# A smaller allowance for filler matmuls between attention units: the TensorE price of a unit in the credit rule goes from 3.6 N to 4.0 N

## The chip, the cores and the metric

The kernel runs on all 8 NeuronCores of one Trainium2 chip, each on one sequence of a batch of 8, with no traffic between cores. The metric is the device time in microseconds (us) of the slowest core. One profiled execution is looked at closely; its page and its finest views are those of core 7, the slowest.

## What is computed

The reference, cut to what matters (layernorm, softmax and silu are the usual ones; 16 heads of 64, sequence 2048, embedding 1024):

```python
xn = _layernorm(x, axis=-1)
q = shape_heads((xn @ wq.T + bq) * scaling)
k = shape_heads(xn @ wk.T + bk)
v = shape_heads(xn @ wv.T + bv)
scores = jnp.einsum('bhtd,bhsd->bhts', q, k)
mask = jnp.triu(jnp.full((T, T), -10000.0, dtype=jnp.float32), k=1)
attn = jax.nn.softmax(scores.astype(jnp.float32) + mask, axis=-1).astype(jnp.float16)
out = jnp.einsum('bhts,bhsd->bhtd', attn, v)
s = out.transpose(0, 2, 1, 3).reshape(B, T, E) @ wo.T + bo
g = _silu(jnp.einsum('bsd,od->bso', xn, weight) + pooled @ disha)
x = x + s * g
```

## The kernel before, in words

**Stages.** Each core first normalizes and transposes its 2048 rows, then runs the projections Q, K (line 345), V (line 370) and the gate g (line 394) as dense matmuls. Then comes attention, and behind it a drain. The change touches only what is issued from attention on.

**Attention.** The queries go in four blocks of 512 (`tc` 0 to 3). Each block runs over the 8 pairs of heads (`p`), and each pair over its chunks of 128 keys (`sc`): 4, 8, 12 and 16 chunks in blocks 0 to 3, since the mask is causal. One step (block, pair, chunk) is called a **unit** here; there are 32 + 64 + 96 + 128 = 320. A unit is a QK of two matmuls, one for each head (L643, L647), with N = 512 columns, or 384, 256 and 128 in the last three chunks of a pair; one exponential of both heads on ScalarE (L656, "exp" below), into one of 7 buffers PT; in the last four chunks a multiplication with the triangle on GpSimd (L665); and a PV of two matmuls (L682, L686), which TensorE issues five units later, out of a queue `pvq`. The QK results lie in two alternating PSUM slots, so QK of unit u waits for exp of unit u-2.

**The end of a pair.** Behind the last PV of a pair VectorE copies both heads' sums out (L575 OddA, L577 OddB), and the first PV of the next pair waits for the second copy, since it writes the same PSUM. SyncE moves the copies into AttnOT, and the softmax sums, one row for each head, into L16. After the eighth pair of a block VectorE takes the reciprocal of L16 (L611).

**The fillers.** Between the units TensorE gets pieces of two kinds of other work, which write the two PSUM slots of Q2. An **N tile** is one matmul (L462, 16 rows of contraction) that spreads the reciprocals, and a multiplication on VectorE that norms one pair's AttnOT (L471). An **E tile** is the output projection of 128 rows by 512 columns: eight matmuls (L505), one for the bias (L510, 1 row of contraction), then on VectorE times g (L520), plus x (L523), and the output DMA from GpSimd (L529) out of two alternating buffers `esb`. Each block has 8 N tiles and then 8 E tiles, and `fillq` holds them in that order, block by block. The N tiles of a block become ready with its reciprocal, its E tiles when its last N tile is done. The x rows for an E tile are loaded on SyncE's queue (L165) when the first E tile of the block is made.

**What sets the order.** The engines' instructions are written out in program order by this code; nothing reorders them at run time. After each unit a credit grows, and each time that it holds `CHUNK = 440.0`, `pop_chunk` takes one chunk: at most two matmuls of the current tile, so one chunk for an N tile and five for an E tile (four pairs and the bias alone). The credit is capped at `CCAP = 2600.0`. The multiplication, addition and output of a finished tile are issued when the next tile begins (`flush_pend`). What is left in `fillq` after the last unit runs in the **drain**:

```python
        while pvq:
            pvq.pop(0)()
            while lnq:
                lnq.pop(0)[1]()

        while fillq or FS["cur"] is not None:
            assert pop_chunk(), "filler not ready at drain"
```

The last reciprocal is thus in VectorE's order ahead of the evacuations of all tiles in the drain. It waits for DMAs that collect the last sums.

Of the kernel before, what the change touches and what calls it, by code (L numbers as in the profile page):

```python
# [44 lines left out]
def build_program(debug=False):  # L45
# [104 lines left out]
    with ExitStack() as ctx:  # L150
# [468 lines left out]
        for tc in range(NTC):  # L619
# [5 lines left out]
            for p in range(NPAIR):  # L625
                for sc in range(nsc):
# [7 lines left out]
                    N = 512 - off  # L634
# [60 lines left out]
                    if len(pvq) >= 5:  # L695
# [1 line left out]
                    pvq.append(pv_e)  # L697
                    u += 1
                    FS["credit"] = min(CCAP, FS["credit"]
                                       + (172.0 + 2 * N) / 1.2 - 3.6 * N / 2.4)  # L700
                    while FS["credit"] >= CHUNK:
                        if not pop_chunk():
                            break
# [104 lines left out]
```

How the kernel before makes its waits and increments, by code:

```python
def build_program(debug=False):  # L45
# [659 lines left out]
        while pvq:  # L705
            pvq.pop(0)()
            while lnq:
                lnq.pop(0)[1]()
        while fillq or FS["cur"] is not None:
            assert pop_chunk(), "filler not ready at drain"
        flush_pend()
        flush_pend()
        for i2 in range(2):
            S.emit("gpsimd", lambda g, i_=i2: g.wait_ge(sems[f"sO{i_}"], last_out[i_]))
        if debug:
            dma("sync", dbg["dbg_AOT"], AttnOT[:],
                waits=[("sDVE", tc_norm[3][0]), ("sSH0", sh_last[0])], sem="sDBG")
            gw = [(s, max((v for s2, v in g_done.values() if s2 == s), default=None))
                  for s in ("sACT", "sDVE")]
            dma("sync", dbg["dbg_g"], g_sb[:], waits=gw, sem="sDBG")
            S.emit("sync", lambda g: g.wait_ge(sems["sDBG"], S.cnt["sDBG"]))
        globals()["_last_cnt"] = dict(S.cnt)
        def run(eng, q):
            lastw = {}
            for fn, waits, inc, amt, _val in S.ops[q]:
                for (s, v) in waits:
                    if lastw.get(s, -1) >= v:
                        continue
                    eng.wait_ge(sems[s], v)
                    lastw[s] = v
                inst = fn(eng)
                if inc is not None:
                    inst.then_inc(sems[inc], amt)
```

## Time and profile before

| | us |
|---|---|
| two timed runs | 778.58 and 806.78 (median 792.68) |
| the profiled execution, whole | 781.28 |
| its span, slowest core (7) | 779.7 |
| spans of the 8 cores | 758.3 to 779.7 |
| PE (TensorE) busy on core 7 | 653.0 |
| ACT (ScalarE) busy | 341.4 |
| DVE (VectorE) busy | 251.7 |

### The profile page before, as it was taken

The numbers are of one execution on the slowest core, as the hardware profiler recorded it, in microseconds if no ns is written. First come the engines' busy times: TensorE is split into PE (matmuls) and PEld (weight loads), VectorE is DVE, ScalarE is ACT, GpSimd is POOL, SyncE is SP. The second block draws the span as 40 slices with busy tenths as digits, with TensorE's granted clock in tenths as the row PEclk, the third lists the DMA queues.
The fourth block names the chain that finished last, engine by engine and source line by source line (L and its number), as shares of the span: only waits on it lengthen the run. The fifth ranks groups of instructions, "written<-read, shape, count | busy, mean of one in ns | idle before, by whom it ended". The sixth has DMA issues, their size and how long they took to land.

```text
span 779.7 us, 8775 instructions; the slowest of 8 cores (758.3 to 779.7 us)
## 1 busy us (share of the span) xinstructions
PE 653.0 (84%) x2784; PEld 238.2 (31%) x2784; DVE 251.7 (32%) x372; ACT 341.4 (44%) x387; POOL 103.1 (13%) x164
## 2 busy tenths in 40 slices
PE   0543999999999999777688889998999899988665
PEld 0433444444333444221122222222222222222211
DVE  5856644444333100022422323222213321222154
ACT  0322000000000233655257788657789858888400
POOL 0000000000000000343022313111131211111201
PEclk9999999999999999755568999659799959999868
DMA  6322410110100000300020111020001120110122
GB/s 199 90 64 67 156 55 1 55 54 7 49 1 0 1 0 1 115 22 21 7 68 28 30 39 48 20 62 28 21 32 38 34 62 21 35 34 21 42 67 95
DMA packets 25696, 34.86 MB, mean 45 GB/s; under 512 B 4898, under 2 KB 19362, under 8 KB 25652
## 3 DMA queue, kind: packets, MB, share of 16 engines
q1 hardware_dynamic: 23092, 25.91, 11.6%
q0 software_dynamic: 2560, 8.39, 2.8%
q8 instruction: 24, 0.39, 0.2%
q14 instruction: 20, 0.16, 0.1%
HBM read 21.63 MB, written 8.39 MB: 39 GB/s over the span
## 4 chain that ended last, share of the span: by engine, by line
PE 73%; DVE 15%; DMA 4%; issue 4%; ACT 1%; SPq 1%; DVEq 1%; POOL 0%; POOLq 0%; ACTq 0%
PE PS L682 14%; PE PS L345 13%; PE PS L643 12%; PE PS L686 9%; PE PS L370 8%; PE PS L394 7%; PE Q L505 6%; DVE OddB L577 3%; DVE OddA L575 3%; DVE xn L233 2%; DVE st L208 1%; DVE st L210 1%; DMA xin<-x 1%; PE Q L462 1%; PE PS L373 1%
## 5 line engine op out<-in xcount | busy, mean ns | idle before, releaser
L656 ACT ACTIVATE PT<-PS,neg 128x1024 f16<-128x1024 f32 (+1 forms) x320 | 300.5, 984 | 113.1 <-PE PS L647 109.0
L665 POOL TENSOR_TENSOR PT<-PT,tri 128x256 f16<-128x256 f16 x128 | 85.9, 677 | 633.1 <-ACT PT L656 628.5
L682 PE MATMUL PS<-PT,Vp 128*65 128x512 f16 (+1 forms) x320 | 135.1, 422 | 41.0 <-DVE OddB L577 40.8
L643 PE MATMUL PS<-QT,KT 64*128 64x512 f16 (+1 forms) x320 | 126.8, 397 | 9.0 <-ACT PT L656 7.9
L686 PE MATMUL PS<-PT,Vp 128*65 128x512 f16 (+1 forms) x320 | 129.7, 405 | 0.0
L647 PE MATMUL PS<-QT,KT 64*128 64x512 f16 (+1 forms) x320 | 127.3, 399 | 0.0
L345 PE MATMUL PS<-xnT,wsb 128*128 128x512 f16 x512 | 112.3, 382 | 0.8 <-DVE QT L355 0.8
L575 DVE CAST OddA<-PS 65x512 f16<-65x512 f32 x32 | 22.0, 687 | 222.4 <-PE PS L686 205.0
L400 ACT ACT_TABLE_LOAD x1 | 1.3, 1283 | 182.4 <-PE PS L394 182.4
L505 PE MATMUL Q<-woT,AttnOT 128*128 128x512 f16 x256 | 77.4, 402 | 1.4 <-DVE AttnOT L471 1.1
L643 PEld LDWEIGHTS PS<-QT,KT 64*128 64x128 f16 x320 | 30.2, 94 | 144.3 <-issue 144.3
L682 PEld LDWEIGHTS PS<-PT,Vp 128*65 128x65 f16 x320 | 36.5, 114 | 117.6 <-issue 112.3
L241 PE MATMUL PS<-eye,xn 128*128 128x128 f32 x128 | 31.0, 424 | 49.1 <-ACT xnT L250 34.6
L345 PEld LDWEIGHTS PS<-xnT,wsb 128*128 128x128 f16 x512 | 50.4, 99 | 62.3 <-issue 3.2
L370 PE MATMUL PS<-wsb,xnT 128*128 128x512 f16 x256 | 60.8, 380 | 0.0
L520 DVE TENSOR_TENSOR esb<-Q,g 128x512 f32<-128x512 f32 x32 | 22.1, 692 | 105.7 <-PE Q L510 71.7
L394 PE MATMUL PS<-Weff,xnT 128*128 128x512 f16 x256 | 55.4, 379 | 0.0
L241 PEld LDWEIGHTS PS<-eye,xn 128*128 128x128 f32 x128 | 25.1, 223 | 54.6 <-issue 54.6
L686 PEld LDWEIGHTS PS<-PT,Vp 128*65 128x65 f16 x320 | 39.6, 124 | 0.3
L382 DVE CAST Vp<-PS 128x512 f16<-128x512 f32 x32 | 22.2, 695 | 46.4 <-PE PS L373 46.4
L505 PEld LDWEIGHTS Q<-woT,AttnOT 128*128 128x128 f16 x256 | 25.1, 101 | 30.4 <-issue 9.7
L394 PEld LDWEIGHTS PS<-Weff,xnT 128*128 128x128 f16 x256 | 25.0, 98 | 30.2 <-issue 0.2
(39 smaller groups left out, 349.4 us busy)
## 6 DMA issues: line engine op xcount, KB each, us to landing
out<-esb POOLq DMA_DIRECT2D x32, 256.0 KB, 2.4
xin<-x SPq DMA_DIRECT2D x16, 256.0 KB, 3.8
wbig<-wT SPq DMA_DIRECT2D x8, 512.0 KB, 6.7
QT<-x SPq DMA_DIRECT2D x32, 128.0 KB, 2.3
wsb<-wqT SPq DMA_DIRECT2D x2, 1024.0 KB, 8.6
wsb<-wkT SPq DMA_DIRECT2D x2, 1024.0 KB, 5.2
wsb<-wvT SPq DMA_DIRECT2D x2, 1024.0 KB, 5.3
woT<-woT SPq DMA_DIRECT2D x1, 2048.0 KB, 10.8
```

Source lines behind the costliest of these rows:

```text
L241: p_tp[tt] = S.emit("tensor", lambda g, jj=j, p=tt % 2: g.transpose(PS6[:, 4 + jj // 4, (jj % 4) * NP:(jj % 4 + 1) * NP], xn_sb[p][:, jj * ...
L345: g.matmul(ps, wsb[w][:, ec_, o_ * NP:(o_ + 1) * NP], xnT[:, ec_, t_ * 512:(t_ + 1) * 512], start=first, stop=last))
L370: g.matmul(ps, xnT[:, ec_, t_ * NP:(t_ + 1) * NP], wsb[w][:, ec_, :], start=first, stop=last))
L394: g.matmul(ps, xnT[:, ec_, t_ * NP:(t_ + 1) * NP], Weff[:, ec_, h * 512:(h + 1) * 512], start=first, stop=last))
L505: S.emit("tensor", lambda g: g.matmul(psF[sl], AttnOT[:, pc_, t_ * NP:(t_ + 1) * NP], woT[:, pc_, o * 512:(o + 1) * 512], start=first, sto ...
L575: evA = S.emit("vector", lambda g: g.tensor_copy(OddA[0:65, :], PS6[0:65, 4, :]), waits=wr, inc="sDVE")
L643: g.matmul(PS6[:, 2 * par_ + 0, o:o + n], KT[0:64, p_, sb2:sb2 + NP], QT[0:64, p_, t + o:t + 512], start=True, stop=True),
L647: g.matmul(PS6[:, 2 * par_ + 1, o:o + n], KT[64:128, p_, sb2:sb2 + NP], QT[64:128, p_, t + o:t + 512], start=True, stop=True),
L656: g.activation(PT[sl_][:, :, o:o + n], PS6[:, 2 * par_:2 * par_ + 2, o:o + n], AF.Exp, bias=neg2[:]), waits=we, inc="sACT")
L665: g.tensor_tensor(PT[sl_][:, :, o:o + NP], PT[sl_][:, :, o:o + NP], t, ALU.mult),
L682: S.emit("tensor", lambda g: g.matmul(psO(0, 65, 0, o, o + n), Vp[:, s_, (2 * p_) * 65:(2 * p_) * 65 + 65], PT[sl_][:, 0, o:o + n], start= ...
L686: pv = S.emit("tensor", lambda g: g.matmul(psO(0, 65, 1, o, o + n), Vp[:, s_, (2 * p_ + 1) * 65:(2 * p_ + 1) * 65 + 65], PT[sl_][:, 1, o:o ...
```

## The change

One number changes: the matmul columns that a unit is charged with.

```diff
                     FS["credit"] = min(CCAP, FS["credit"]
-                                       + (172.0 + 2 * N) / 1.2 - 3.6 * N / 2.4)
+                                       + (172.0 + 2 * N) / 1.2 - 4.0 * N / 2.4)
```

The first term stands for the unit's exponential, the second for its matmuls, both in ns. Before, a unit adds 228.7, 207.3, 186.0 or 164.7 (N = 512, 384, 256, 128); now it adds 143.3 whatever N is. So a pair of block 3 is given 8.0 chunks before and 5.2 now, one of block 2 5.9 and 3.9, one of block 1 3.9 and 2.6. All the work remains; its places change.

In TensorE's order before, inside block 3, a filler (L505 x2) stands two units after the one ahead of it:

```order
1280 L505 MATMUL Q<-woT,AttnOT 128x512 x2
1281 L643 MATMUL PS<-QT,KT 128x512
1282 L647 MATMUL PS<-QT,KT 128x512
1283 L682 MATMUL PS<-PT_61,Vp 65x512
1284 L686 MATMUL PS<-PT_61,Vp 65x512
1285 L643 MATMUL PS<-QT,KT 128x512
1286 L647 MATMUL PS<-QT,KT 128x512
1287 L682 MATMUL PS<-PT_62,Vp 65x512
1288 L686 MATMUL PS<-PT_62,Vp 65x512
1289 L505 MATMUL Q<-woT,AttnOT 128x512 x2
```

In TensorE's order of the change, in the same block, three units follow on a filler before the next one, which is the row L510 directly below these:

```order
1272 L505 MATMUL Q<-woT,AttnOT 128x512 x2
1273 L643 MATMUL PS<-QT,KT 128x512
1274 L647 MATMUL PS<-QT,KT 128x512
1275 L682 MATMUL PS<-PT_61,Vp 65x512
1276 L686 MATMUL PS<-PT_61,Vp 65x512
1277 L643 MATMUL PS<-QT,KT 128x512
1278 L647 MATMUL PS<-QT,KT 128x512
1279 L682 MATMUL PS<-PT_62,Vp 65x512
1280 L686 MATMUL PS<-PT_62,Vp 65x512
1281 L643 MATMUL PS<-QT,KT 128x512
1282 L647 MATMUL PS<-QT,KT 128x512
1283 L682 MATMUL PS<-PT_63,Vp 65x512
```

Fillers have moved apart, from every second unit to every third.

TensorE's order at the end of attention before: behind the last PV come the 8 N tiles and then the 8 E tiles of block 3.

```order
1504 L682 MATMUL PS<-PT_110,Vp 65x128
1505 L686 MATMUL PS<-PT_110,Vp 65x128
1506 L462 MATMUL Q<-L_57,hsel 128x512 x8
1507 L505 MATMUL Q<-woT,AttnOT 128x512 x8
1508 L510 MATMUL Q<-bo_sb,ones_76 128x512
```

The same place in the change, first the beginning of the drain and then its middle:

```order
1458 L682 MATMUL PS<-PT_110,Vp 65x128
1459 L686 MATMUL PS<-PT_110,Vp 65x128
1460 L462 MATMUL Q<-L_57,hsel 128x512 x6
1461 L505 MATMUL Q<-woT,AttnOT 128x512 x8
1462 L510 MATMUL Q<-bo_sb,ones_76 128x512
```

```order
1475 L505 MATMUL Q<-woT,AttnOT 128x512 x8
1476 L510 MATMUL Q<-bo_sb,ones_76 128x512
1477 L462 MATMUL Q<-L_57,hsel 128x512 x8
1478 L505 MATMUL Q<-woT,AttnOT 128x512 x8
1479 L510 MATMUL Q<-bo_sb,ones_76 128x512
```

Six N tiles and all eight E tiles of block 2 now stand in the drain, ahead of those of block 3.

Over the whole of attention TensorE now has 18 N tiles and 16 E tiles between its units where it had 24 and 24. The N tiles of block 1 stood at units 128 to 142 (one at each second) and now stand at units 172 to 192 (one at each third); those of block 2 stood at units 225 to 238, and now two stand at the end of block 3 and six in the drain.

VectorE's order at the end of attention before:

```order
228 L575 CAST OddA<-PS 65x512
229 L577 CAST OddB_85<-PS 65x512
230 L611 RECIPROCAL L_57<-L_57 16x512
231 L471 TENSOR_TENSOR AttnOT<-AttnOT,Q 128x512 x8
232 L520 TENSOR_TENSOR esb_47<-Q,g 128x512
```

And in the change:

```order
211 L575 CAST OddA<-PS 65x512
212 L577 CAST OddB_85<-PS 65x512
213 L611 RECIPROCAL L_57<-L_57 16x512
214 L471 TENSOR_TENSOR AttnOT<-AttnOT,Q 128x512 x7
215 L520 TENSOR_TENSOR esb_47<-Q,g 128x512
```

The evacuations of the moved tiles stand behind the last reciprocal; the first L471 among them belongs to an N tile whose matmul is still inside attention. On SyncE's queue the 8 loads of x for block 2 (L165) move from the middle of block 3 to the end, next to the 8 for block 3.

## Rows read from the trace of the kernel before

**Rows 1.** The cores view: span and mean granted clock of a core.

```profile
core 5: 758.6 us, clock 0.920
core 7: 779.7 us, clock 0.890
```

**Rows 2.** TensorE's timeline, core 7, at the full clock: start, duration, engine, line.

```profile
480.12 0.39 PE L510 MATMUL Q<-bo_sb,ones 1*128 1x512 f16 x1
480.44 0.39 PE L643 MATMUL PS<-QT,KT 64*128 64x512 f16 x1
...
485.03 0.38 PE L686 MATMUL PS<-PT,Vp 128*65 128x512 f16 x1
485.35 0.39 PE L643 MATMUL PS<-QT,KT 64*128 64x512 f16 x1
...
485.91 0.38 PE L686 MATMUL PS<-PT,Vp 128*65 128x512 f16 x1
486.12 0.59 PE L505 MATMUL Q<-woT,AttnOT 128*128 128x512 f16 x2
486.65 0.39 PE L643 MATMUL PS<-QT,KT 64*128 64x512 f16 x1
```

**Rows 3.** ScalarE's timeline, core 7, behind the end of a pair.

```profile
668.28 2.12 ACT L656 ACTIVATE PT<-PS,neg 128x1024 f16<-128x1024 f32 x2 [1.24 <-PE PS L647]
```

**Rows 4.** TensorE's timeline, core 7, at the lower clock.

```profile
407.01 0.63 PE L686 MATMUL PS<-PT,Vp 128*65 128x512 f16 x1
407.44 1.06 PE L505 MATMUL Q<-woT,AttnOT 128*128 128x512 f16 x2
408.43 0.60 PE L643 MATMUL PS<-QT,KT 64*128 64x512 f16 x1
...
409.39 0.63 PE L686 MATMUL PS<-PT,Vp 128*65 128x512 f16 x1
409.96 0.60 PE L643 MATMUL PS<-QT,KT 64*128 64x512 f16 x1
```

**Rows 5.** Stretches of core 7: length, busy time of each engine, PEclk, DMA.

```profile
100.00:300.00 200.00, 200.00 (x897) 84.79 (x896) 64.88 (x87) 13.86 (x23) 0.00 (x0) 1.00 0.07 22
320.00:380.00 60.00, 40.73 (x146) 10.71 (x146) 16.37 (x20) 30.79 (x39) 23.21 (x35) 0.51 0.17 50
490.23:510.37 20.14, 18.74 (x54) 4.00 (x54) 5.51 (x9) 12.25 (x14) 3.17 (x5) 0.55 0.06 20
510.37:528.95 18.58, 17.04 (x57) 4.24 (x57) 4.12 (x7) 11.37 (x13) 2.67 (x4) 0.66 0.22 64
540.00:548.00 8.00, 6.10 (x23) 1.72 (x22) 2.76 (x4) 5.21 (x6) 0.00 (x0) 0.72 0.09 20
574.57:587.81 13.24, 12.13 (x59) 3.86 (x59) 2.76 (x5) 11.32 (x13) 3.68 (x6) 1.00 0.14 50
623.30:648.12 24.82, 23.28 (x75) 5.50 (x75) 5.50 (x9) 16.31 (x18) 2.66 (x4) 0.66 0.17 48
684.00:701.89 17.89, 16.34 (x78) 5.17 (x78) 4.14 (x7) 15.51 (x18) 3.68 (x6) 1.00 0.11 37
```

**Rows 6.** A stretch of core 5: from OddB of one pair to OddB of the next.

```profile
628.86:646.74 17.88, 16.34 (x78) 5.16 (x78) 4.14 (x6) 15.56 (x18) 3.15 (x5) 1.00 0.07 23
```

**Rows 7.** The timeline of the drain, core 7.

```profile
740.54 3.34 DVE L611 RECIPROCAL L<-L 16x512 f16<-16x512 f16 x1 [3.71 <-DMA L<-OddB]
...
744.85 6.25 DVE L471 TENSOR_TENSOR AttnOT<-AttnOT,Q 128x512 f16<-128x512 f16 x8 [0.97 <-PE Q L462]
...
751.35 3.57 PE L505 MATMUL Q<-woT,AttnOT 128*128 128x512 f16 x8 [1.12 <-DVE AttnOT L471]
...
755.34 1.90 PE L505 MATMUL Q<-woT,AttnOT 128*128 128x512 f16 x8
...
764.17 1.89 PE L505 MATMUL Q<-woT,AttnOT 128*128 128x512 f16 x8 [0.17 <-DVE esb L520]
...
768.69 1.89 PE L505 MATMUL Q<-woT,AttnOT 128*128 128x512 f16 x8 [0.16 <-DVE esb L520]
```

## The prediction, made before the changed kernel was run

> **What bounds the kernel now.** Look first at the cores [rows 1]: the same program takes 758.6 us on core 5 and 779.7 on core 7, and the slower one has the lower mean clock. So TensorE is near enough to the limit that its clock shows in the time, and the kernel's time is that of the core whose clock fell most.
>
> Then at one unit at the full clock. From an L686 to the next QK it is 0.32 us without a filler (485.03 to 485.35), and 0.56 later comes the next L686 (485.91): a unit with N = 512 costs TensorE 0.88 us [rows 2]. ScalarE's exp of such a unit takes 2.12 / 2 = 1.06 us [rows 3]. Without fillers ScalarE would set the pace. A pair of L505 lengthens the step from L686 to QK from 0.32 to 0.74 us, so it costs 0.42; a single L510 (and, by the same row, an L462) costs its 0.32 [rows 2]. With one chunk in about two units, four in five of them pairs, TensorE needs 0.88 + 0.52 x 0.40 = 1.09 us a unit, only 0.03 over ScalarE's pace. The two engines are almost balanced.
>
> Last at the pairs of heads. One of block 3 takes 17.89 us at the full clock on core 7, and 17.88 on core 5, with ScalarE busy 15.51 and idle 2.4 [rows 5, 6]. Half of that idle time is one gap of 1.24 us at the pair's end [rows 3]. With the clock down the same 16 units took 24.82 us [rows 5].
>
> **The change, part by part.** Eight E tiles (32 pairs of L505, 8 single L510) and six N tiles (6 single L462) leave attention for the drain: 46 chunks.
>
> *What attention gains.* At the full clock, if TensorE kept the pace, 32 x 0.42 + 14 x 0.32 = 17.9 us [rows 2]. ScalarE's pace lies close under it, so not all can be had. In a pair of block 3 the 2.8 chunks removed are 1.1 us of TensorE's time. The 13 long units can give 0.03 each, 0.4; the rest must come out of ScalarE's idle 2.4 us: the gap at the pair's end, when no filler stands in it any more, and the three short units, whose exps are shorter than TensorE's work. I take 0.9 to 1.0 of the 1.1, or 85%: 15 us. At the lower clock a pair of L505 costs 1.42 - 0.57 = 0.85 us [rows 4], twice as much, and TensorE alone sets the pace. By core 7's mean clock of 0.890 some 170 us of its span were at the lower level [rows 1]; block 0, before the first filler, has 59 of them [rows 5] and the drain a part, so I estimate that a fifth of the chunks lie in such stretches: 0.2 x 18 = 4 us more. Together -19 us. Bounds: -12, if only the long units' 0.4 and half of the rest come; -26, if half of the chunks removed had stood at the lower clock.
>
> *What the drain pays.* Nothing but its own DMAs runs beside it, so all of it is on the path. VectorE reaches the moved evacuations only behind the reciprocal, which waits for the last sums: the 3.71 us of that wait and the 3.34 of L611 are not filled [rows 7], except by the matmul or two that fit in the two PSUM slots. Behind it:
> - Seven L471 of block 2's N tiles at 6.25 / 8 = 0.78: 5.5, less the 0.97 that the first now waits for its matmul [rows 7]: 4.5 us.
> - The first E tile at the lower clock, 755.34 - 751.35 = 4.0, and seven at (768.69 - 764.17) / 2 = 2.26, the pace of the two output buffers [rows 7]: 19.8.
> - Block 3's first L471 then waits for the last E tile's L520 and L523: about 1.5.
>
> Sum +26 us. Bounds: 23, if the first tile runs at the full clock and TensorE's 1.90 + 0.32 a tile is the pace; 30, if the clock falls again among these tiles. Block 3's own tiles cost what they did. The 16 loads of x, now in a row on SyncE, are issued while VectorE waits for the reciprocal and then works through N tiles; I cost them at nothing, since the second eight are wanted only 26 us later, and the first eight have the reciprocal and 5.5 us of L471 to land in. In the middle of block 3 eight loads disappear from ahead of OddA's and OddB's DMAs, for which nobody waits there: nothing.
>
> On a limit by current the trace says this: through 200 us of dense matmuls on eight cores PEclk is 1.00 [rows 5]. The Trainium skill (TensorE: Matmul & The Clock Gate, Part 1, Seeing it yourself) says that once three cores of a die run dense matmuls a limiter takes the clock to 13/16. By it each of the eight moved tiles would take some 2.7 us in the denser drain, 3 to 4 us more in all; the trace disagrees, and the sum doesn't need it.
>
> *The clock.* This is the term that no row prices directly. With N tiles as fillers the clock stays down: 20.14 and 18.58 us for pairs of block 2 at 0.55 and 0.66, against 13.24 for one at 1.00, an excess of 12 us; at block 2's N tiles in block 3 24.82 instead of 17.88 us, 6.9 us, on core 7 but not on core 5 [rows 5, 6]. With none (block 0) it is 0.51, and one fall came in block 2 among E fillers, with 0.72 in its 8 us [rows 5]. The clock comes back around E fillers: the steps at 407 to 410 are at the lower clock, L505 among them [rows 4], those at 485 at the full one [rows 2]. So full-height fillers hold the clock up, and the change thins them from one chunk in two units to one in three. Against that, attention's own matmuls then come a little faster, and only one stretch of N tiles is left inside blocks 2 and 3 instead of two, 21 units long instead of 14. I price: the second stretch gone, -7; the first longer by half of its excess, +6; one or two more falls among E fillers on the slowest core at 3 to 7 us each, +7. Sum +6 us. Bounds: -10 (no such falls, a quick recovery) and +35 (half of the 24 pairs lose 3 us each).
>
> **Sum.** 781.28 (the profiled execution, 1.6 us more than its span) - 19 + 26 + 6 = 794; I say 793 us, 1.5% more than before. The two runs of before are 778.58 and 806.78; the profiled one agrees with the lower, and the median 792.68 is only their middle. My percentages are against 781. About 2%, to 797 or 766, is what a measurement of this kernel can tell from no change.
>
> **The rivals.**
> - *The clock gives way.* At one chunk in three units the falls at the pairs' ends become the rule. For it: block 0's 0.51 and the fall at 540 [rows 5], at a denser filling than will be. Against it: the pairs late in block 3 hold 1.00 [rows 5, 6]. A pair of block 3 that loses the clock loses up to 6.9 us; if a third to a half of the 24 pairs of blocks 1 to 3 lose 3 us on average, that is 24 to 36 instead of my 7: 810 to 822.
> - *ScalarE swallows the gain.* If its idle time at the pairs' ends doesn't shrink, since OddB's copy and not the filler sets it, a pair gives back only the long units' 0.4, some 8 us in all, and 4 of the lower clock: 781 + 26 - 12 + 6 = 801, or 796 with half of the clock's term.
> - *Faster.* The second N stretch leaves attention and takes the slowest core's fall with it; fewer matmuls among the rest do no harm. Core 5, which never fell there, ended 21 us earlier [rows 1]. If every core becomes like core 5: 758.6 + 1.6 + 26 - 15 = 771, and with the first N stretch no more costly than now and gains at pair ends in full, 765. It decides at the point where thirds of fillers still hold the clock.
> - *The change doesn't do what it says.* The order shows the tiles in the drain; no chance.
>
> **How the numbers follow.** The forecast, 785 to 797: 0.46. The clock gives way: 0.30. ScalarE swallows the gain: 0.12, of which 0.08 over the line of 797. Faster: 0.12, of which 0.07 under 766. So slower by over 2% 0.38, within 2% 0.46 + 0.04 + 0.05 = 0.55, faster 0.07. The range, 770 to 824, takes in all but the far end of the first rival and the larger part of the last.
>
> **What the changed profile would show.** From L611's start to the end of the span 39.2 us before (779.7 - 740.54); 64 to 67 if the drain's price is right. A pair of block 3 at the full clock 16.8 to 17.1 us instead of 17.89, with ScalarE idle 1.3 to 1.6. Seven L471 behind L611 without a gap. In the granted clock one long low stretch, in the last part of block 2, instead of two; and at the pairs' ends elsewhere either no more falls than now, or many. I am wrong if the pairs at the full clock don't shorten (ScalarE), if the moved tiles run at under 2 us each or hide in the wait for the reciprocal, or if the slowest core's mean clock moves by more than 0.02: 0.02 of the span is 31 us more or less at the lower level, where a pair takes 1.39 times as long, some 9 us.

## The result, and the profile after

The change makes the kernel slower by half a per cent: 783.79 us against 779.65 (medians of 30 and 29 runs), and the ratio of the comparable runs is 1.0053, with a 95% interval of 1.0035 to 1.0071. The direction was the forecast one, the size was not: +4 us instead of +12. The profiled executions are 779.75 us for the change and 781.28 before, one 4 us under its median and one 1.6 over, so the traces are compared part by part and not by their ends. (On every chip some executions run with part of the cores at a lower granted clock for long, 0.75 through the dense matmuls in one of delay_3_6, an experiment below; they are left out, and so are cores 6 and 7 of delay_only below.)

The cores of the changed kernel; these are its slowest and fastest:

```profile
core 1: 778.2 us, clock 0.916
core 2: 772.1 us, clock 0.918
```

Before, they lay between 758.6 and 779.7 [rows 1]. The spread has shrunk from 21 us to 6: the mean of the eight spans rose by 6.3 us (768.8 to 775.1), the slowest hardly moved.

From the starts of L577, the copy at each pair's end, every core's span splits into blocks (from the eighth such start, the end of block 0, to the sixteenth and so on) and the part behind the last one. Means over the eight cores, in us:

| | block 1 | block 2 | block 3 | sum | behind the last OddB |
|---|---|---|---|---|---|
| before | 90.8 | 123.0 | 145.0 | 358.8 | 43.3 |
| change | 92.2 | 108.3 | 136.0 | 336.5 | 71.6 |
| difference | +1.4 | -14.7 | -9.0 | -22.3 | +28.3 |

So attention gave back 22 us, and the drain took 28, in these two executions.

The drain, VectorE's timeline on core 1:

```profile
710.86 3.34 DVE L611 RECIPROCAL L<-L 16x512 f16<-16x512 f16 x1 [3.71 <-DMA L<-OddB]
714.30 5.46 DVE L471 TENSOR_TENSOR AttnOT<-AttnOT,Q 128x512 f16<-128x512 f16 x7
724.43 0.69 DVE L520 TENSOR_TENSOR esb<-Q,g 128x512 f32<-128x512 f32 x1 [4.67 <-PE Q L510]
...
741.48 0.69 DVE L520 TENSOR_TENSOR esb<-Q,g 128x512 f32<-128x512 f32 x1 [1.31 <-DMA out<-esb]
...
743.07 6.25 DVE L471 TENSOR_TENSOR AttnOT<-AttnOT,Q 128x512 f16<-128x512 f16 x8
```

The wait of 3.71 us ahead of L611 is as long as before [rows 7]. Seven L471 follow without a gap, then eight E tiles whose evacuations start at 724.43 for the first and 741.48 for the last, 2.44 us apart; only then come block 3's eight L471. From L611 to the end it is 67.3 us (778.2 - 710.86), where it was 39.2.

TensorE's timeline in the same stretch shows the clock within it:

```profile
720.01 3.57 PE L505 MATMUL Q<-woT,AttnOT 128*128 128x512 f16 x8 [1.11 <-DVE AttnOT L471]
724.05 2.60 PE L505 MATMUL Q<-woT,AttnOT 128*128 128x512 f16 x8
726.90 1.90 PE L505 MATMUL Q<-woT,AttnOT 128*128 128x512 f16 x8
...
737.65 1.90 PE L505 MATMUL Q<-woT,AttnOT 128*128 128x512 f16 x8
...
749.58 3.46 PE L505 MATMUL Q<-woT,AttnOT 128*128 128x512 f16 x8 [1.12 <-DVE AttnOT L471]
```

The first eight matmuls take 3.57 us, at the lower level, the second eight still 2.60, and the clock is lost once more while block 3's N tiles run, so the price of a restart is paid twice.

Attention on core 1, pair by pair (from OddB to OddB; after the five engines' busy times comes PEclk):

```profile
487.59:500.66 13.07, 11.44 (x56) 3.68 (x56) 2.76 (x5) 11.10 (x14) 2.58 (x4) 1.00 0.04 10
526.59:540.96 14.37, 12.77 (x54) 3.67 (x54) 2.77 (x5) 11.43 (x13) 3.68 (x6) 0.88 0.14 47
553.54:569.93 16.39, 14.56 (x55) 3.72 (x55) 4.13 (x7) 11.74 (x14) 2.62 (x4) 0.79 0.30 74
569.93:588.31 18.38, 16.81 (x73) 4.87 (x73) 6.10 (x5) 15.49 (x18) 3.03 (x4) 0.91 0.03 8
605.33:624.02 18.69, 17.21 (x75) 5.04 (x75) 2.76 (x4) 15.45 (x17) 3.15 (x5) 0.91 0.07 22
657.68:674.77 17.09, 15.39 (x73) 4.78 (x73) 2.75 (x5) 15.24 (x17) 3.11 (x5) 1.00 0.08 25
```

At the full clock a pair of block 3 now takes 17.09 us with ScalarE busy 15.24, against 17.89 [rows 5]. The three long pairs of before, 20.14, 18.58 and 24.82 us at 0.55 to 0.66 [rows 5], have no counterpart in blocks 2 and 3 of this core. The lowest there is the last pair of block 2, at 0.79, in which the one N stretch ends. On core 0, alone of the eight, that pair is still a long one:

```profile
552.45:571.26 18.81, 17.27 (x55) 4.05 (x55) 4.13 (x6) 11.98 (x14) 2.67 (x4) 0.64 0.25 64
```

What came instead are short falls, pairs at 0.88 to 0.91 that lose some 1.5 us. The first pair of block 1 is as it was, 21.47 us at 0.54 on core 1 against 22.01 at 0.50 on core 7 before; what it holds comes out below.

### The profile page after: what moved, and what is told of

Its sections match the earlier page's. It is cut to its first block, busy times and chain, and to the rows that moved or that the text cites. A ratio compares the mean times of both kernels' runs of the same rounds, so it can differ in the third digit from the quotient of the medians.

```text
span 778.2 us, 8777 instructions; the slowest of 8 cores (772.1 to 778.2 us)
## 1 busy us (share of the span) xinstructions
PE 639.3 (82%) x2784; PEld 237.4 (31%) x2784; DVE 251.5 (32%) x372; ACT 335.9 (43%) x387; POOL 102.4 (13%) x164
## 4 chain that ended last, share of the span: by engine, by line
PE 66%; DVE 16%; DMA 5%; issue 5%; ACT 4%; SPq 1%; DVEq 1%; POOL 0%; ACTq 0%; POOLq 0%
PE PS L345 13%; PE PS L682 12%; PE PS L643 10%; PE PS L370 8%; PE PS L686 8%; PE PS L394 7%; PE Q L505 5%; ACT PT L656 4%; DVE OddB L577 3%; DVE OddA L575 3%; DMA out<-esb 2%; DVE AttnOT L471 2%; DVE xn L233 2%; DMA xin<-x 2%; DVE st L208 1%
## 5 line engine op out<-in xcount | busy, mean ns | idle before, releaser
L656 ACT ACTIVATE PT<-PS,neg 128x1024 f16<-128x1024 f32 (+1 forms) x320 | 295.0, 989 | 88.1 <-PE PS L647 86.1
L682 PE MATMUL PS<-PT,Vp 128*65 128x512 f16 (+1 forms) x320 | 128.7, 402 | 41.4 <-DVE OddB L577 41.3
L643 PE MATMUL PS<-QT,KT 64*128 64x512 f16 (+1 forms) x320 | 120.9, 379 | 13.4 <-ACT PT L656 11.2
L686 PE MATMUL PS<-PT,Vp 128*65 128x512 f16 (+1 forms) x320 | 122.8, 384 | 0.0
L647 PE MATMUL PS<-QT,KT 64*128 64x512 f16 (+1 forms) x320 | 121.9, 382 | 0.0
L505 PE MATMUL Q<-woT,AttnOT 128*128 128x512 f16 x256 | 75.6, 411 | 3.3 <-DVE AttnOT L471 2.5
L682 PEld LDWEIGHTS PS<-PT,Vp 128*65 128x65 f16 x320 | 35.8, 112 | 112.9 <-issue 107.3
L686 PEld LDWEIGHTS PS<-PT,Vp 128*65 128x65 f16 x320 | 38.0, 119 | 0.4
L505 PEld LDWEIGHTS Q<-woT,AttnOT 128*128 128x128 f16 x256 | 25.0, 103 | 35.4 <-issue 16.0
```

Source lines behind the costliest of these rows:

```text
L505: S.emit("tensor", lambda g: g.matmul(psF[sl], AttnOT[:, pc_, t_ * NP:(t_ + 1) * NP], woT[:, pc_, o * 512:(o + 1) * 512], start=first, sto ...
L643: g.matmul(PS6[:, 2 * par_ + 0, o:o + n], KT[0:64, p_, sb2:sb2 + NP], QT[0:64, p_, t + o:t + 512], start=True, stop=True),
L647: g.matmul(PS6[:, 2 * par_ + 1, o:o + n], KT[64:128, p_, sb2:sb2 + NP], QT[64:128, p_, t + o:t + 512], start=True, stop=True),
L656: g.activation(PT[sl_][:, :, o:o + n], PS6[:, 2 * par_:2 * par_ + 2, o:o + n], AF.Exp, bias=neg2[:]), waits=we, inc="sACT")
L682: S.emit("tensor", lambda g: g.matmul(psO(0, 65, 0, o, o + n), Vp[:, s_, (2 * p_) * 65:(2 * p_) * 65 + 65], PT[sl_][:, 0, o:o + n], start= ...
L686: pv = S.emit("tensor", lambda g: g.matmul(psO(0, 65, 1, o, o + n), Vp[:, s_, (2 * p_ + 1) * 65:(2 * p_ + 1) * 65 + 65], PT[sl_][:, 1, o:o ...
```

## The experiments

Theory A, from these rows: a filler with all 128 rows of contraction (L505) brings TensorE's clock back and a low one (16 rows in L462, 1 in L510) doesn't; the change gained in attention by shortening the long low stretches, and not because thinner fillers are cheap. The rivals: the clock falls by the gap at a pair's end, whatever fills (D); the gain comes from the thinner fillers themselves (H). The drain's price is told apart from all of that by moving one instruction.

Where the clock falls and rises can be read from the kernel before, on core 7. At the end of a pair TensorE waits 1.26 us for OddB and works on; some 1.5 us later its clock falls, and it stays down over the two pairs with N tiles:

```profile
491.06 0.38 PE L682 MATMUL PS<-PT,Vp 128*65 128x512 f16 x1 [1.26 <-DVE OddB L577]
```

```profile
491.00:492.00 1.00, 0.94 (x5) 0.33 (x5) 0.00 (x0) 0.27 (x1) 0.00 (x0) 1.00 0.00 0
492.00:493.00 1.00, 1.00 (x4) 0.14 (x2) 0.69 (x1) 0.60 (x1) 0.00 (x0) 0.70 0.45 113
493.00:494.00 1.00, 1.00 (x4) 0.29 (x4) 0.69 (x1) 0.71 (x2) 0.00 (x0) 0.50 0.09 20
...
522.00:523.00 1.00, 1.00 (x3) 0.15 (x1) 0.00 (x0) 0.00 (x0) 0.67 (x1) 0.50 0.00 0
523.00:524.00 1.00, 1.00 (x5) 0.23 (x4) 0.00 (x0) 0.32 (x1) 0.00 (x0) 0.94 0.00 0
```

It comes back at 523, behind the first pair of L505 that follows the N tiles:

```profile
522.20 1.05 PE L505 MATMUL Q<-woT,AttnOT 128*128 128x512 f16 x2
```

In blocks 2 and 3 of this core and of core 1 of the change there are nine falls. Each begins 0.7 to 2.5 us after the start of L577 at the end of a pair.

Times in the table are medians, with the ratio to the kernel before on the same chip.

| kernel | us | ratio (95%) | block 1 | block 2 | block 3 | behind |
|---|---|---|---|---|---|---|
| price_3_2 | 787.06 | 1.0116 (1.006 to 1.0172) | 91.9 | 120.2 | 155.5 | 43.8 |
| price_4_4 | 809.59 | 1.0393 (1.0297 to 1.0488) | 90.6 | 123.4 | 134.5 | 84.4 |
| n_full | 773.6 | 0.9936 (0.9903 to 0.9969) | 93.3 | 114.2 | 145.9 | 46.1 |
| n_low | 790.67 | 1.011 (0.9973 to 1.0246) | 92.9 | 122.9 | 146.1 | 45.6 |
| interleave | 773.34 | 0.994 (0.9902 to 0.9978) | 91.5 | 115.3 | 149.0 | 43.3 |
| delay_inter | 753.6 | 0.9688 (0.9586 to 0.9791) | 85.0 | 108.5 | 139.1 | 48.3 |
| delay_only (time: delay_3_6) | 758.18 | 0.9756 (0.9699 to 0.9814) | 83.6 | 111.9 | 139.1 | 44.3 |
| delay_4_0 | 781.19 | 1.0069 (1.0043 to 1.0095) | 87.1 | 114.9 | 134.7 | 70.6 |
| late_recip | 776.83 | 1.0003 (0.9966 to 1.0039) | 92.8 | 108.9 | 135.8 | 64.8 |
| all_4_0 | 773.79 | 0.9975 (0.9933 to 1.0017) | 87.4 | 112.9 | 135.5 | 65.3 |
| mix_3_8 | 761.04 | none | 83.7 | 106.9 | 137.1 | 57.0 |
| n_full_4_0 | 788.67 | none | 95.2 | 109.8 | 134.6 | 74.5 |

The parts are means over the eight cores of the profiled execution, for delay_only over cores 0 to 5; they are compared with the one profile of the kernel before, from another chip. The time and ratio in delay_only's line are those of delay_3_6, the same kernel. mix_3_8 and n_full_4_0 have no ratio, and their time is that of the profiled execution alone.

### More and less credit

```diff
-                                       + (172.0 + 2 * N) / 1.2 - 3.6 * N / 2.4)
+                                       + (172.0 + 2 * N) / 1.2 - 3.2 * N / 2.4)
```

> More credit, 314 ns for a long unit, 0.71 chunks. Attention can't hold more than the 144 chunks that it had before, so they come earlier and the end of each block of units runs without fillers until the next reciprocal. Part behind the last OddB 43 us as before. Theory A: in the stretches without fillers the clock falls, as with N tiles, so blocks 2 and 3 together take as long as before or up to 10 us more (268 to 278 us), time 778 to 790. Theory B gives the same sign. Rival C (the clock plays no part, ScalarE against TensorE is all): units with fillers 1.17 us, units without 1.06, sum unchanged, time within 3 us of before.

787 us, 1.2% slower. Block 2 takes 120 us and block 3 155.5, 10 more than before, with the drain unchanged. The numbers are inside what A said, but not for A's reason. These are the first pair of block 3 on core 1 and one late in the block, which has no filler at all:

```profile
578.00:609.80 31.80, 24.74 (x85) 6.14 (x85) 11.60 (x14) 16.09 (x17) 3.21 (x5) 0.68 0.14 38
682.92:700.32 17.40, 15.11 (x64) 4.16 (x64) 1.37 (x2) 15.24 (x17) 2.59 (x4) 0.90 0.03 8
```

The fillers ran out 15 units before the end of block 2, and then five N tiles in a row waited for the reciprocal, 4.93 us in one piece. That first pair alone is 14 us longer than before. The pair without fillers has only a short fall, so in block 3 the clock doesn't stay down for want of fillers (in block 0, which has none either, it is at 0.51 [rows 5]).

With 4.4 in the same place:

> Half as many chunks again leave attention: 58 ns of credit for a long unit and up to 122 for a short one, some 51 chunks in attention in all instead of 98. Theory A (TensorE's clock is held up by full-height fillers and falls where they are missing; one chunk in three units was still enough): one in seven is not enough, pairs at the full clock are at ScalarE's pace (16.5 us in block 3, against 16.9 with 4.0), but the clock falls at most pair ends and block 3 takes over 145 us instead of 136. Theory B (the clock falls only where N tiles or nothing fill, and any E filler holds it): block 3 takes 132 to 134 us. The part behind the last OddB grows from 71.6 by 47 chunks, some 9 tiles of 2.3 us plus N tiles, to 95 to 98. Time: A 810 to 825, B 795 to 800.

3.9% slower. A is wrong about block 3, and B, which had 132 to 134 us for it, comes within half a us of the 134.5 measured. Neither had the rest: the part behind grows only to 84.4 us, because block 3 can't start before block 1's N tiles are done: the code forces 26 chunks in between, and the last pair of block 2 takes 30 us on core 1. In block 3, with one filler in seven units, a pair at the full clock is down to 16.4 us, ScalarE's pace with its gap. Core 1, its first and third pair there:

```profile
575.38:593.02 17.64, 15.72 (x68) 4.44 (x68) 4.72 (x4) 15.08 (x16) 2.58 (x4) 0.90 0.03 8
...
611.21:627.60 16.39, 14.34 (x68) 4.35 (x68) 2.76 (x5) 15.23 (x17) 2.58 (x4) 1.00 0.04 9
```

So thin fillers cost falls of 1.2 to 3 us at the ends of three or four of block 3's eight pairs, and no collapse. And beyond 4.0 there is little left to win: 16.4 against 17.0 us a pair.

### Is it the filler's height?

n_full, in the N tile of the kernel before:

```diff
+                S.emit("tensor", lambda g: g.matmul(
+                    psF[sl], woT[:, 0, 0:NP], woT[:, 0, 0:512],
+                    start=True, stop=True), waits=pw_ + [("sWO", c_wo)])
                 pval = S.emit("tensor", lambda g: g.matmul(
```

> The kernel before, with one additional matmul of 128 rows by 512 columns ahead of each N tile's matmul of 16 rows, into the same PSUM slot, overwritten by it: 32 more matmuls, 24 in attention, 0.21 us each at the full clock, some 5 us of TensorE's time. Theory A (low fillers let the clock fall, full-height ones hold it): the falls at the N tiles of blocks 1 and 2 go, block 2 takes 110 to 114 us instead of 117 to 125, block 3 139 to 141 on every core instead of 148 on most; time 8 to 12 us less than before. Rival D (it falls by the gap at the pair's end, whatever fills the units): block 2 and 3 unchanged or 2 us longer each, time +3 to +5.

n_low has the N tile's own 16-row matmul in that place instead:

> Control for n_full: the kernel before, with each N tile's own matmul of 16 rows issued twice instead of once behind a matmul of 128 rows. The same number of matmuls with the same columns, but low ones. Theory A (it is the height of the filler that holds TensorE's clock): block 2 takes 117 to 125 us on the cores and block 3 140 to 149, as before, and the part behind the last OddB 46; time 3 to 6 us more than before. Rival E (any matmul more between the units holds it): block 2 114 us as in n_full, time 5 us less than before.

With the high one block 2 falls from 123.0 to 114.2 us, with the low one it stays at 122.9. Both kernels have the same number of matmuls with the same columns. The pair with the N stretch and the one behind it on core 1, n_full:

```profile
487.82:503.47 15.65, 14.11 (x59) 4.02 (x59) 5.51 (x8) 11.65 (x14) 3.15 (x5) 0.89 0.08 26
503.47:517.53 14.06, 12.52 (x60) 4.01 (x60) 4.12 (x6) 11.33 (x13) 2.63 (x4) 1.00 0.30 84
```

and n_low:

```profile
492.05:512.08 20.03, 18.48 (x59) 3.96 (x59) 5.51 (x8) 11.87 (x14) 3.17 (x5) 0.66 0.06 21
512.08:530.59 18.51, 16.96 (x60) 4.21 (x60) 4.12 (x7) 11.54 (x13) 2.67 (x4) 0.72 0.21 64
```

Seven of n_full's eight cores have the same two pairs to 0.05 us. In n_low one of the two or both are at 0.56 to 0.72, on every core. So in block 2 the height tells and the mere number doesn't. But a high filler doesn't bring the clock back each time. On core 0 of n_full the first of these pairs, and on core 7 the pair with the second N stretch, are as long as those of before or longer:

```profile
488.81:508.90 20.09, 18.54 (x59) 4.52 (x59) 5.51 (x9) 11.86 (x14) 3.17 (x5) 0.66 0.07 21
```

```profile
611.57:639.04 27.47, 25.92 (x80) 6.27 (x80) 5.50 (x9) 16.12 (x17) 2.66 (x4) 0.63 0.14 43
```

On core 7 the clock stood at 0.50 from 614 to 633 us, with a full-height matmul ahead of each of the N tiles in between, and came back behind the first pair of L505 (L508 there), as before. In block 3 neither kernel gave what A said: 145.9 and 146.1 us. Its pair with the second N stretch takes 20.1 to 27.5 us in n_full, in n_low 20.1 on five cores and 29.0 on three, in the kernel before 17.5 on three and 24.8 on five. So there the height isn't shown to do anything. n_full's time fell by 0.6%, half of what was expected. That is the slowest core's: the mean of the eight spans over its comparable executions is 766.2 us, against 766.7 before and 776.5 for n_low, whose two such executions leave its ratio unclear.

In n_full_4_0 the same edit stands in the change:

> The change (4.0) with n_full's edit: a full-height matmul ahead of each N tile's low one. In the change one N stretch is left inside blocks 2 and 3, in the last two pairs of block 2, and block 2 has 7.0 us above eight times its shortest pair. Theory A (height holds the clock): that excess falls to 2 to 4, block 2 takes 103 to 105 us; blocks 1 and 3 as in the change (92 and 136); time 1 to 4 us less than that of the change, since 14 of the 32 additional matmuls are in the drain. Rival F (the excess in the change is from its thin E fillers, not from the N tiles): block 2 stays at 107 to 109, time 1 to 3 us more than the change.

Block 2 takes 109.8 us instead of 108.3, nearer to F, with an excess over the shortest pairs of 5.4 to 6.6 us on four cores and 10.9 to 12.0 on the other four. So in the change the 7 us in the last pairs of block 2 are not cured by high N fillers. The cause is open.

### N tiles between E tiles

interleave takes an N tile between two chunks of an E tile, when one is ready, from `pop_chunk`; its core is:

```diff
+            if FS["cur"] is not None and FS["cur_kind"] == "E":
+                k = next((i for i, e_ in enumerate(fillq) if e_["kind"] == "N"), None)
+                if FS["alt"] and k is not None and fillq[k]["ready"]():
...
+                    em_n = mk_n_tile(fillq.pop(k))[0]
```

> The kernel before with its credit; the N tiles of a block are not issued in a row, but one by one between the chunks of the E tiles of the block before that are still left, so that an N tile stands at most at every fourth unit. The same matmuls in attention and drain. Theory A: no stretch without full-height fillers is left behind block 1's, so block 2 takes 106 to 110 us (eight pairs of 13.25), block 3 139 to 141 on all cores; time 10 to 14 us less than before. Rival D: no change, within 3 us.

0.6% faster, again half of the expectation. Block 2 gains 8 us, block 3 loses 4. The two long stretches are gone from core 1, but new ones stand at the first pair of blocks 2 and 3:

```profile
460.44:480.03 19.59, 13.91 (x57) 3.94 (x57) 7.47 (x7) 11.35 (x13) 3.20 (x5) 0.83 0.03 7
480.03:493.45 13.42, 11.87 (x57) 3.71 (x57) 3.44 (x6) 11.52 (x14) 2.62 (x4) 1.00 0.10 31
...
574.82:599.73 24.91, 18.64 (x76) 5.22 (x76) 8.17 (x9) 16.11 (x18) 3.66 (x5) 0.86 0.05 17
```

In the first, TensorE is busy 13.91 of 19.59 us, which a low clock doesn't explain: it stands still, for the reciprocal (L623 here):

```profile
468.32 0.58 PE L462 MATMUL Q<-L,hsel 16*128 16x512 f16 x1 [4.28 <-DVE L L623]
```

An N tile is "ready" as soon as the reciprocal has been issued, not when it is done, and TensorE, in order, waits for it.

### A wait that all versions had

The kernel before stands so too, in the first pair of block 1, here on core 7:

```profile
376.92 1.00 PE L462 MATMUL Q<-L,hsel 16*128 16x512 f16 x2 [4.80 <-DVE L L611]
```

delay_inter and delay_only hold N tiles back for ten units:

```diff
-                                  ready=(lambda t=tcq: lambda: norm_meta[t] is not None)()))
+                                  ready=(lambda t=tcq: lambda: norm_meta[t] is not None
+                                         and u >= n_at[t])()))
...
+                            n_at[tc_] = u + 10
```

> As interleave, with 3.6, but an N tile is taken at the earliest ten units after its block's reciprocal was issued, so that TensorE doesn't wait for L611 in its order. In interleave the first pair of block 3 took 24.9 us on core 1, against 17.8 in the kernel before. If that was this wait, block 3 takes 141 to 143 us instead of 149, and block 1, where the kernel before has the same wait, 84 to 88 instead of 91; time 10 to 14 us less than interleave, 760 to 764. Rival: the fall of the clock in that pair has another cause, and block 3 keeps over 147.

> The kernel before with 3.6, N tiles in a row as there, but none before ten units after its reciprocal. It splits what delay_inter gained. If the delay and the interleaving each pay for themselves: block 1 85 us instead of 91 (TensorE no longer waits for L611 there), block 2 117 to 125 and block 3 140 to 148 as before, since the N stretches remain; time 4 to 7 us less than before, 771 to 774. Rival: the delay alone does it all, blocks 2 and 3 come down to 110 and 140 as well, and the time is 753 to 758.

delay_inter is 3.1% faster than before, the best of all, and 20 us under interleave where 10 to 14 were expected. The split came out as the rival of delay_only had it, for blocks 2 and 3 too: the delay alone brings 83.6, 111.9 and 139.1 us, 24 of the 26 us. The first pair of block 1 takes 22.0 us in interleave and, in the kernel before, the same to the tenth; here are that pair on core 0 of delay_only, the next one, and the pair of block 2 that holds most of the first N stretch:

```profile
368.36:377.98 9.62, 7.77 (x32) 2.09 (x32) 4.72 (x4) 6.99 (x8) 2.67 (x4) 0.82 0.06 14
377.98:393.57 15.59, 13.62 (x40) 2.92 (x40) 5.50 (x8) 7.74 (x10) 2.72 (x5) 0.58 0.04 10
...
493.42:506.32 12.90, 11.60 (x54) 3.43 (x54) 4.82 (x7) 11.13 (x12) 2.83 (x5) 1.00 0.10 32
```

The two pairs of block 1 together take 25.2 us instead of 33.7. The N stretch of block 2 runs at 1.00 here and on four more of the six cores read. On core 3 it is low, as on all eight cores before:

```profile
494.13:512.56 18.43, 17.14 (x54) 3.91 (x54) 4.82 (x7) 11.40 (x12) 2.87 (x5) 0.63 0.07 22
```

So A has to be narrowed. A row of low fillers doesn't bring the clock down by itself: the second one of the kernel before also ran at 1.00 on three cores (17.66 and 17.54 us for its two pairs on core 0). The falls come at pairs' ends, and what fills behind them has a part in how long they last. Moved by eight units, the same stretch mostly misses the fall. That this is what spared block 2, and not the missing wait in block 1, is argued from where the pairs lie: no run has the one without the other.

### The change once more, on that kernel

delay_3_6 (the same kernel as delay_only) and delay_4_0 ran on one chip:

> The same kernel as delay_only (3.6, N tiles in a row, none before ten units after its reciprocal), as the partner of delay_4_0 on the same chip and for its own verdict: block 1 84, block 2 107 to 113, block 3 138 to 140, part behind the last OddB 44; 750 to 756 us, 3% under before.

> The change (4.0) with the same delay; its drain is that of the change. Compared with delay_3_6 it is the change once more, on a kernel that hardly has long stretches at the lower clock. Theory G (the change's attention gained 22 us in the mean because it lost such a stretch, and only some 11 from its units at the full clock): here attention gains only 5 to 12 us, the drain pays 28, and it is 2 to 3% slower than delay_3_6: block 1 84 to 88, block 2 105 to 109, block 3 134 to 137, behind the last OddB 71 to 72, 770 to 776 us. Rival H (the thinner fillers give attention 20 us by themselves): 758 to 764 us, within 1.3% of delay_3_6.

3.6 gives 758.18 us and 4.0 gives 781.19, 3.0% more by these medians and 3.2% by the two ratios. Attention doesn't get shorter at all: 83.6 + 111.9 + 139.1 = 334.6 us with 3.6, 87.1 + 114.9 + 134.7 = 336.7 with 4.0. Theory G had 5 to 12 us of gain and was still too kind; H is out. Block 3 gains 4.4, and blocks 1 and 2 lose 3.5 and 3.0. Block 2 loses it in one pair, its last, where the code forces four N tiles through at once: 21.84 us at 0.61, 8.8 more than a pair at the full clock, and 5.4 more than the change's 16.39. Without the 8.8 attention would gain some 7 us (an estimate), inside what G said and far from H's 20. Core 0 of delay_4_0, a pair at full clock, the last of block 2, and one of block 3:

```profile
494.16:507.22 13.06, 11.32 (x55) 3.58 (x55) 1.37 (x2) 11.09 (x13) 3.10 (x5) 1.00 0.10 32
546.02:567.86 21.84, 19.13 (x58) 4.28 (x58) 6.19 (x10) 12.21 (x14) 2.66 (x4) 0.61 0.22 55
...
603.25:620.42 17.17, 15.70 (x75) 4.83 (x75) 2.76 (x4) 15.26 (x17) 3.15 (x5) 1.00 0.08 24
```

### The drain

late_recip, in the change:

```diff
         while pvq:
             pvq.pop(0)()
-            while lnq:
-                lnq.pop(0)[1]()
+        while n_left[2] > 0:
+            assert pop_chunk()
+        assert pop_chunk()
+        while lnq:
+            lnq.pop(0)[1]()
```

> The change, with one thing moved: the last reciprocal stands in VectorE's order behind the N tiles of block 2 and ahead of the first E tile's evacuation, instead of ahead of all of them. If the drain's price is what was predicted (nothing fills the 3.71 us of the wait for the sums and the 3.34 of L611, because of the order), the part behind the last OddB falls from 71.6 to 64 to 66 us, and the time is 6 to 8 us less than that of the change, 772 to 776, about 1% under the kernel before or even with it. Rival: the collecting DMAs or the x loads behind them set the drain, and it takes 69 to 71.

The part behind the last OddB falls from 71.6 to 64.8 us, as expected, and the time to 776.83, even with before (1.0003). VectorE's timeline on core 1 starts with:

```profile
706.85 0.69 DVE L577 CAST OddB<-PS 65x512 f16<-65x512 f32 x1
707.64 5.45 DVE L471 TENSOR_TENSOR AttnOT<-AttnOT,Q 128x512 f16<-128x512 f16 x7
713.20 3.34 DVE L611 RECIPROCAL L<-L 16x512 f16<-16x512 f16 x1
717.77 0.69 DVE L520 TENSOR_TENSOR esb<-Q,g 128x512 f32<-128x512 f32 x1 [1.23 <-PE Q L510]
```

The seven L471 fill the wait for the sums, and L611 lies beside the first E tile's matmuls. That is the 7 us that the prediction called unfilled because of the order.

> With the change's 4.0: N tiles between E tiles, ten units' delay, and in the drain the reciprocal behind one chunk of an E tile, the last N tiles between the following E tiles' chunks. Attention: block 1 84 to 90, block 2 103 to 105, block 3 134 to 137. Part behind the last OddB: 17 tiles at 2.2 to 2.3 us and few us more, 50 to 56, since waits, reciprocal and N tiles lie beside matmuls. Time 742 to 758 us. Then sparser fillers pay, once the drain hides what it waits for. If it takes 770 or more, the drain's pace is set by something that the tiles don't show, the output DMAs or x.

all_4_0 missed by far: 773.79 us, not 742 to 758. Its drain takes 65.3 us, no less than late_recip's. On core 1 TensorE stands still for 5.17 us while VectorE is busy with the reciprocal, and the eight N tiles between E chunks then run at the lower clock. The DMAs are not what made it late: the last 14 tiles are evacuated 2.27 us apart. Block 2 with thin fillers takes 112.9.

> 3.8, with delay_inter's two edits, and with the last reciprocal behind the first chunk of an E tile in the drain; the five E tiles of block 2 left there fill the wait for it, and block 3's N tiles follow in a row. Attention as in delay_inter or up to 4 us less (85, 107, 137 us), if two chunks in five units hold the clock; the part behind the last OddB 48.3 + 4.7 tiles of 2.25 - 7 for what is hidden = 51 to 53. Time 748 to 756, with delay_inter's 753.6 inside. Rival: at this density blocks 2 and 3 already lose the clock more often, as in all_4_0 (112.9 and 135.5), and the time is 758 to 765.

mix_3_8 has the shortest attention of all, 327.7 us, but behind it 57.0 instead of 51 to 53: on core 1 TensorE stands still for 6.93 us and starts again at the lower clock. Its one time, 761.04, missed the 748 to 756. The mean span of its cores is 752.8, that of delay_inter 747.4. So the rival was right about the time and wrong about blocks 2 and 3, and there is still no gain in thinning, since the drain takes it back.

## Why the prediction was off

**The bounds at work.** Right. At the full clock the two engines are nearly balanced: a pair of block 3 shortened from 17.89 to 17.09 us (16.8 to 17.1 predicted, with ScalarE idle 1.3 to 1.6; it was 1.85), and with half the fillers gone once more only to 16.39.

**What attention gains at the full clock.** Right in size. Comparing pairs at 1.00 on core 1 of the change with those of before, block 3 gives some 0.9 us a pair and block 2 some 0.7, 13 us in all with the little of block 1; 15 were predicted, and 4 more for chunks at the lower clock.

**What the drain pays.** +28.3 us measured, +26 predicted. The 2 us are the second E tile, which still began at the lower clock (2.60 us for its eight matmuls), and tiles 2.44 instead of 2.26 apart. That nothing hides in the wait for the reciprocal was right, and late_recip showed why. The limiter of which the Trainium skill speaks (TensorE: Matmul & The Clock Gate, Part 1, Seeing it yourself) doesn't show in the denser drain either: its L505 x8 take the same 1.90 us as before [rows 7], once the clock is up.

**The clock: the step that failed.** The prediction put it as "+6 us": -7 for the second N stretch, +6 for the longer first one, +7 for more falls. Measured, with the full-clock part of 13 taken out of the 22.3, attention gained 9 more in the mean, where +6 with the 4 us for low-clock chunks makes +2. Between the slowest cores, for which the term was written, it is more: attention took 367.2 us on core 7 before and 337.6 on core 1 of the change, 29.6 less, 17 of them beyond the full-clock part. The slowest core's mean clock rose from 0.890 [rows 1] to 0.916; 0.02 was the prediction's own sign of being wrong. Two terms were mis-sized. The first N stretch was to lose half as much again, and it lost half as much: block 2's excess over its shortest pairs fell from 11.5 to 18.9 us on the cores to 6.4 to 11.7, it seems because at its new place the fall came later and fewer units were left in it. And the additional falls, though they came, were worth 1.5 to 2.5 us each and not 3 to 7. The second stretch's -7 was near: block 3 took 148.3 us on five cores before and 133.6 to 136.6 now, 12 less or more, of which some 7 are the full clock's part. That an N stretch as such keeps the clock low, and full-height fillers hold it up, was a misreading of mine: delay_only runs one at 1.00, and n_full's core 7 stays low for 19 us with high ones. The falls begin at pairs' ends. How long one lasts depends on the fillers in block 2, by n_full against n_low; in block 3 it isn't shown.

**The slowest core.** The time is that of the core with the worst luck, and the change took away falls that only some cores had (block 3: 139.6 to 148.4 us before, 133.6 to 136.6 now), so the slowest core's time rose less than the mean did. Many executions say it more firmly than the two profiled ones. In 21 of the change the eight spans have a mean of 776.5 us and the slowest 780.9. In 13 of the kernel before, on the chip of the first experiments and with nearly the same median (779.29), they are 766.7 and 776.6. The mean core pays about 10 us and the slowest 4. That the first is near the forecast is luck, since the forecast was for the slowest. The profiled pair, with 6.3 for the mean, shows the change too kindly by some 3 us, which the parts above can't place.

**Two sums in the prediction.** In the rival on ScalarE, half of the clock's term makes 798 us, not 796. And the 1.39 at the end is read from a pair at 0.66, of which only two thirds were at the lower level: some 17 us of the 24.82 cost 6.9. So 31 us at the lower level are worth about 13 us and not 9. By the same estimate the slowest core's time at the lower level, 171 us before and 131 after (twice 0.110 and 0.084 of its span), shrank by what is worth 17 us, the figure above.

The half per cent is then, in us and for the profiled pair: 28 for the drain, -13 for less filler work between units, and -9 in the mean for less time at the lower clock; that makes +6 in the mean of the cores. On the slowest the last term is -17, and the medians, 4 us apart, lie between. That the last term came from where the N stretches fell and not from the thinning is what delay_4_0 speaks for. On a kernel without the wait at L611 the same edit costs 3%, a part of it by the four forced N tiles. Not settled: why a pair's end brings the clock down on one core and not on another, and what decides how long it stays down.

## What to carry to other kernels

A rule that only moves work has its price where the work lands: put a number on the drain before thinning what fills the body. In a program order fixed in advance, "issued" is not "done": a consumer placed right behind its producer's issue stops its whole engine, and ten units of distance were worth 2.4% here, over four times the effect under study (7 of the 24 us lie in block 1, where the wait was; the rest came with the new places of the fillers). And when a change gains where its own arithmetic gives nothing, repeat it on a kernel without the suspected accident, before crediting the change.

## What the hardware showed that was not expected

- Between otherwise equal kernels, a 128-row matmul beside each 16-row filler brought TensorE's granted clock back (pairs at 0.89 and 1.00, 15.65 and 14.06 us), and a second 16-row one didn't (0.66 and 0.72, 20.03 and 18.51 us). That is block 2, on seven of eight cores; in block 3 a core stayed at 0.50 for 19 us with the 128-row ones (27.47 us).
- The clock fell within 0.7 to 2.5 us after the copy at a pair's end, where TensorE had waited 1.26 us, and pairs without any filler lost only a little (17.40 us at 0.90 in price_3_2).
- A stretch of 16-row fillers that begins at the full clock can stay there: 12.90 us for a pair at 1.00 in delay_only, on five of the six cores read (18.43 at 0.63 on the sixth).
- The cores of one chip run the same attention in blocks of nearly the same few lengths (block 2 before: 117.4 us on two, 124.8 on six), as if each coincidence were taken or missed whole.
